# Reordering the steps, GpSimd shares, gathers and loads of a three-layer interaction network

## What is computed

```python
e = stack([tbl_f[ids[:, f]] for f in range(32)], axis=1)       # 512 x 32 x 16
x0 = xk = e
for W in (W0, W1, W2):                                         # 32 x (32 or 64) x 64
    xk = relu(einsum('bmd,bhd,mhk->bkd', x0, xk, W))           # 512 x 64 x 16
    outs.append(sum(xk, axis=2))
h = concatenate([*outs, dense_ctx], axis=1)                    # 512 x 208
y = relu(relu(h @ W_top1 + b1) @ W_top2 + b2) @ W_top3
```

## Time and profile before

| | before |
|---|---|
| median of 3 runs | 338.52 us |
| profiled execution: its time / its span | 339.5 us / 337.7 us |
| granted TensorE clock, mean | 0.98 |
| TensorE matmul busy | 309.4 us (92%) |
| VectorE busy | 268.5 us (80%) |
| GpSimd busy | 240.6 us (71%) |
| ScalarE busy | 63.1 us (19%) |
| DMA, mean rate over the span | 188 GB/s |

### The profile page before, as it was taken

The page is one execution under the profiler, slowest core; times in us unless marked ns, Lnnn a source line. Parts: engine busy times, 40 slices in busy tenths (PEclk is TensorE's granted clock), DMA queues, the critical chain, the costliest instruction groups (busy, mean ns, idle before and its releaser), DMA issues.

```text
span 337.7 us, 4699 instructions
## 1 busy us (share of the span) xinstructions
PE 309.4 (92%) x1828; PEld 128.8 (38%) x1828; DVE 268.5 (80%) x162; ACT 63.1 (19%) x103; POOL 240.6 (71%) x186
## 2 busy tenths in 40 slices
PE   0469999878989998989999999999999999999997
PEld 0435456434545353323333333333333333333334
DVE  0128579937996699999999999999998979999210
ACT  1030322122113410101221301131132012020011
POOL 5677777777777358899979797979958577649200
PEclk9998999995899999999999999999999999999999
DMA  6366647366398409696979696915998995230000
GB/s 176 106 178 175 214 109 224 73 170 203 98 308 304 156 10 320 213 307 196 325 246 308 247 322 200 330 45 151 317 363 259 320 284 135 36 103 1 2 0 0
DMA packets 31356, 63.60 MB, mean 188 GB/s; under 512 B 5606, under 2 KB 13030, under 8 KB 31334
## 3 DMA queue, kind: packets, MB, share of 16 engines
q1 hardware_dynamic: 20614, 52.28, 46.7%
q10 hardware_dynamic: 6624, 9.96, 10.1%
q0 software_dynamic: 4096, 1.06, 3.3%
HBM read 51.35 MB, written 1.71 MB: 157 GB/s over the span
## 4 chain that ended last, share of the span: by engine, by line
PE 58%; DMA 5%; DVE 2%; issue 1%; ACT 0%; SPq 0%; DVEq 0%
PE acc L951 51%; DMA fields_sb<-fields 5%; DVE vz L741 2%; PE factor L996 2%; PE acc L964 1%; PE factor L906 1%; PE factor L991 1%; PE factor L1003 1%; PE acc L996 1%; PE factor L1037 0%; PE acc L1074 0%; ACT factor L787 0%; SPq L611 0%; DVE feats L751 0%; DVE vz L772 0%
## 5 line engine op out<-in xcount | busy, mean ns | idle before, releaser
L741 DVE TENSOR_TENSOR vz<-fields_sb,factor 128x1024 f32<-128x1024 f32 (+3 forms) x113 | 230.5, 2089 | 31.9 <-PE factor L906 15.6
L951 PE MATMUL acc<-vz,w_sb 128*64 128x512 f32 (+1 forms) x1152 | 216.3, 514 | 7.9 <-DVE vz L741 7.2
L669 POOL DMA_INDIRECT gathered<-in_table,index x128 | 121.7, 951 | 38.4 <-issue 36.0
L686 POOL TENSOR_TENSOR pz<-fields_sb,hidden 128x1024 f32<-128x1024 f32 (+1 forms) x52 | 118.1, 2295 | 33.0 <-DMA hidden<-relu_out 9.5
L951 PEld LDWEIGHTS acc<-vz,w_sb 128*64 128x64 f32 x1152 | 82.2, 140 | 127.3 <-issue 89.9
L951 PE MATMUL acc<-pz,w_sb 128*64 128x512 f32 (+1 forms) x208 | 50.6, 578 | 0.0
L853 ACT ACTIVATE relu_out<-acc 128x512 f32<-128x512 f32 (+1 forms) x30 | 15.5, 516 | 109.9 <-PE acc L951 104.3
L787 ACT ACTIVATE factor<-hidden 128x1024 f32<-128x1024 f32 (+1 forms) x23 | 20.1, 879 | 59.7 <-DMA hidden<-relu_out 38.1
L741 DVE TENSOR_TENSOR vz<-rotated,factor 128x2048 f32<-128x2048 f32 x10 | 22.5, 2279 | 5.3 <-ACT factor L787 5.3
L951 PEld LDWEIGHTS acc<-pz,w_sb 128*64 128x64 f32 x208 | 15.0, 137 | 28.8 <-issue 26.5
L751 DVE TENSOR_REDUCE feats<-relu_out 128x32 f32<-128x512 f32 (+1 forms) x30 | 17.1, 570 | 6.6 <-ACT relu_out L853 6.5
(11 more groups left out here) (30 smaller groups left out, 43.0 us busy)
## 6 DMA issues: line engine op xcount, KB each, us to landing
fields_sb<-fields SPq DMA_DIRECT2D x48, 512.0 KB, 5.5
rotated<-fields SPq DMA_DIRECT2D x20, 512.0 KB, 6.7
fields_sb<-fields SPq DMA_DIRECT2D x32, 256.0 KB, 3.6
hidden<-relu_out ACTq DMA_DIRECT2D x30, 256.0 KB, 5.8
own<-fields SPq DMA_DIRECT2D x5, 512.0 KB, 3.6
gathered<-in_table,index POOLq DMA_INDIRECT x128, 3.7
hidden<-relu_out ACTq DMA_DIRECT2D x16, 128.0 KB, 3.8
fields<-gathered SPq DMA_DIRECT2D x5, 256.0 KB, 4.9
```

Source lines behind the costliest of these rows:

```text
L669: nc.gpsimd.indirect_dma_start(gathered[:, pair % GRING, j, :], None, table, bass.IndirectOffsetOnAxis(ap=index[:, i:i + 1], axis=0)).then ...
L686: nc.gpsimd.tensor_tensor(pz[:, at % PRING, 0:cols], fields[s][:, t, col:col + cols], hidden_of(step, g), ALU.mult).then_inc(pz_ready, 1)
L741: nc.vector.tensor_tensor(vz[:, at:at + nt, 0:cols].rearrange("p t (a n) -> p t a n", n=half), src[:, t:t + nt, col:col + cols].rearrange( ...
L951: last = nc.tensor.matmul(acc_of(step, ab), weights[:, kt, :], z[:, ab * half:(ab + 1) * half], start=start and j == 0, stop=stop and j == ...
```

## The change

Only tables and one constant change: the order BEGUN, the sets SPREAD, HALF and PAIRED, the shares POOL_TILES, the places of the gathers, the waits PACED and BEHIND_SPREAD on gathers, the order LOADS, and the place at which ScalarE makes the own squares of layer 0.

- BEGUN: (0, 2) comes ahead of (2, 0), (0, 3) ahead of (1, 1), and (0, 4) ahead of (2, 1) rather than behind (2, 2). (0, 6) comes ahead of (2, 4), (0, 7) ahead of (2, 5), and (2, 6) ahead of (0, 8).
- SPREAD and HALF: five spreads of both halves become four, seven of one half become six.
- GpSimd's tiles: 52 become 56. Two narrow steps that had a share, (1, 1) with 1 and (2, 3) with 3, have none, (1, 3) has 1, and the wide steps have 55 rather than 48; (1, 4) has 4 rather than 1, (2, 8) has 6 rather than 3.
- PAIRED: in (2, 2) the tiles are contracted alternately into the two halves of the accumulator, in one matmul of 512 columns instead of two of 256; ScalarE copies the accumulator out (`fold`), and TensorE adds the halves (`join`) before the relu.
- PACED gives 84 gathers a wait, BEHIND_SPREAD 8.
- LOADS: the scratch of block 3 ahead of that of block 2, that of block 5 ahead of that of block 4, and that of block 6 ahead of the fields of block 5.

```diff
-BEGUN = [(0, 0), (1, 0), (0, 1), (2, 0), (0, 2), (1, 1), (1, 2), (0, 3), (2, 1), (1, 3), (2, 2), (0, 4), (0,
+BEGUN = [(0, 0), (1, 0), (0, 1), (0, 2), (2, 0), (0, 3), (1, 1), (1, 2), (0, 4), (2, 1), (1, 3), (2, 2), (0,
...
-SPREAD = [(1, 0), (2, 3), (1, 4), (1, 5), (1, 9)]
-HALF = [(1, 1), (2, 0), (1, 2), (1, 3), (2, 4), (1, 7), (2, 7)]
+SPREAD = [(1, 0), (1, 3), (2, 2), (1, 7)]
+HALF = [(2, 0), (1, 1), (1, 2), (1, 5), (2, 4), (2, 5)]
...
-FIRST_GATHERS = 21
-GATHERS_IN = {(1, 1): (14,), (2, 3): (48, 0, 1), (1, 4): (2,), (1, 5): (10, 0, 0, 2, 0), (2, 4): (3, 0, 0),
+FIRST_GATHERS = 40
+GATHERS_IN = {(1, 3): (29,), (1, 4): (21, 6, 1, 0), (1, 5): (3, 0, 0, 2), (2, 4): (0, 1, 3), (2, 5): (3, 4, 1,
...
-PACED = {}
+PACED = {11: 2, 12: 2, 13: 2, 14: 2, 15: 3, 16: 3, 17: 4, 18: 4, 19: 3, 21: 3, 22: 2, 24: 6, 25: 3, 26: 4, 27:
...
-PAIRED = []
+PAIRED = [(2, 2)]
...
-            due.append((COLUMNS[VECTOR.index((step, 0))] + TURN_LAG, "own", step, 0))
+            due.append((COLUMNS[VECTOR.index((step, 0))], "own", step, 0))
```

## The result

The kernel after takes **336.70 us** (median of 12 runs, 334.56 to 338.02) against 338.64 for the kernel before in the same comparison: a ratio of 0.9933, 95% interval 0.9903 to 0.9962, so it is faster, by 1.9 us between the medians. 334.1 was forecast: the direction was right, the size less than half. Medians are over all runs of a kernel; the ratios leave out single slow runs, such as one of 1344.38 us among the twelve of the kernel before. The profiled execution of after took 337.33 us with a span of 335.5; before 339.5 and 337.7.

A forecast was written before the change was run, and what follows sets the result against it. TensorE's start of (1, 5) and its work from there bound the kernel, with GpSimd at (1, 4) the new bound. -5.5 - 1.1 + 2.2 = -4.4 gave 335.1 profiled, 334.1 median; range 330.3 to 338.9, own range 332 to 336.3.

The forecast's parts named there:

- TensorE reaches (1, 5) at 140.3: End of (1, 4): GpSimd's products set TensorE's start of (1, 5), at 140.3 rather than 145.81, 5.5 us earlier.
- gives gather 68 at 91.1, the product of (1, 3): GpSimd's queue at 1.25 per gather, walked on to the four products of (1, 4), ending 121.9, 131.6, 135.1 and 137.5.
- Without these waits (1, 4) would end near 136.5: TensorE in (1, 4): it waits for GpSimd about 3 us in all; otherwise the step ends near 136.5.
- The rule on the clock: TensorE's half rate would move rather than vanish; priced at +1.0, with only VectorE late.
- Head: VectorE ahead of (1, 5): begins (2, 0) at 41.7, (1, 1) at 55.3, (2, 1) at 79.2, ends (2, 3) at 121.5.
- rival C: 63 gathers up to number 96: new waits stretch the issue gap, 0.14 more each gives 342.9; chance 0.12.
- Rival A: At (1, 4) GpSimd is no bound: it ends at 136.5, 328.1 at most, 331 likelier; chance 0.14.
- From (1, 5) on: From (1, 5) to the perceptron: TensorE's work, 173.5 before, changes by -1.1 and +2.2.
- +2.2: GpSimd late by 0.7 at the first product of (1, 5), 1.5 at the fifth of (2, 5); bounds nothing and 5.
- -1.1: TensorE from (1, 5) on: one spread fewer, -1.07.
- Rival B: GpSimd's late products in (1, 5) to (1, 7) hold the loads of fields 6 and 7: 337.6; chance 0.18.
- PAIRED and LOADS: PAIRED at (2, 2) costs 0; LOADS delays block 2's fields to about 51 to 60, used at 64, not in the sum.

The follow-up runs named there:

- experiment 11: Kernel after without waits on gathers, two gathers moved from ahead of (1, 5)'s first product to ahead of (1, 4)'s second: 337.55 us.
- experiment 4: Kernel after with four entries in the ring of relu outputs instead of three: 335.47 us.
- experiment 2: Kernel after with PACED and BEHIND_SPREAD emptied, so no waits on gathers: 334.91 us.
- experiment 3: Kernel after with ten idle matmuls on TensorE ahead of the contraction of (0, 2), their values overwritten: 335.83 us.
- experiment 9: Kernel after with the old order LOADS: 336.36 us.
- experiment 5: Kernel after with experiments 1, 2 and 3 together: 334.18 us.
- experiment 10: Kernel after with experiments 1 to 4 together: 334.03 us.
- experiment 8: Kernel after without waits on gathers and with (0, 4) put back behind (2, 2): 338.57 us.
- experiment 7: Kernel after with PAIRED emptied, so (2, 2) has neither fold nor join: 336.67 us.
- experiment 1: Kernel after with the one product of (1, 3) moved from GpSimd to VectorE, its 29 gathers put into (1, 4): 336.01 us.

## Why the prediction was right and wrong

**TensorE reaches (1, 5) at 140.3: failed, 142.55.** The mechanism was right. In eight profiles the start of (1, 5) follows GpSimd's first product of (1, 4) by 20.95 to 21.00 us, whatever made that product early or late, and two gathers more put 2.48 us into that distance (experiment 11). What failed is the step at which the queue alone "gives gather 68 at 91.1, the product of (1, 3)", with nothing down for its hidden operand, and with it the times of the four products of (1, 4): 139.6 for 137.5. Of the 2.1 us 0.4 are gather 11, 1.25 late instead of 0.8. 1.7 are the wait for the hidden copy. My walk has no relu of (0, 4) between the squares and the copy, and so overlooks that it must wait for the entry of the relu ring, hence for the spread of (1, 3), hence for VectorE; and it puts nothing down for the four relays between relu and copy, which took 4.94 us to issue. The wait is gone with a fourth entry (experiment 4) and in the profiles of the same ring with 1.00 at 42 us (experiments 2 and 3), and it is 0.24 us where the relays took 3.43 (experiment 9).

**"Without these waits (1, 4) would end near 136.5": wrong by the prediction's own prices.** 16 tiles at 0.863 are 13.8 us, and behind VectorE's first unit at 124.8 they end at 138.6. The runs show this distance as 13.77 us. In after it makes 140.50, so even without GpSimd's waits (1, 5) would have been 0.2 later than forecast.

**"GpSimd holds (1, 4) at 140.3 anyway": failed.** The rule on the clock was priced at +1.0 on the ground that only VectorE would be late. Half rate at 42 us came true, in six of the nine profiles without idle matmuls, and it moved GpSimd too, through the very copy above. In the profile of after this is 1.7 us at (1, 5); in that of experiment 9 GpSimd waits 0.24. I weighed it as a thing that happens or not, while it comes and goes between executions.

**Head.** The start of (2, 0) was forecast 1.1 too late, the waits behind (0, 4) were right: 4.88 ahead of (2, 1) for 4.8, none at (0, 5). With the clock at 1.00 VectorE starts (2, 1) at 78.39, for 79.2.

**Waits on gathers, rival C: false.** The pitch is 1.25 with them. What they cost is 1.2 us at gather 11, for 0.8 forecast (by the medians 1.8 without the fourth relu output and 1.0 with it). **Rival A** was false as well: GpSimd did bound (1, 4), and it was out of the way only in experiments 5, 10 and 8. It was also priced too high: ahead of (1, 5) it could give 140.3 - 138.6 = 1.7 us, not 3.8.

**From (1, 5) on: right in sum, its parts not shown.** 174.65 for 174.6. The forecast +2.2 was to be waits for `pz` in (1, 5), (2, 5) and (1, 7). In after TensorE waits once for `pz`, 0.43 at 145.71, and 0.70 for VectorE at 278.74; the chain gives that one back to the last gathers of block 9 (223.41), its scratch and its loads. The rest is a gap of 0.11 at 185.38, and next to nothing elsewhere. TensorE is busy for 173.37 us of this part, against 173.53 before, and idle for 1.28, against nothing. By this count the terms are -0.2 and +1.3 rather than -1.1 and +2.2, though the ends of matmuls are modelled, so that part of a pause can be counted as work. That one spread fewer is worth 1.07 was not tested by itself. In the other eleven profiles the part takes 173.1 to 175.0 us. So the agreement of the sum to 0.05 us is luck. In the walk itself, from (1, 5) to (2, 5) the tables give 12 products and 20 gathers, not 16 and 23; the 53 us fit the former (28.2 + 25).

**Rival B** (337.6), late products that hold the loads of fields 6 and 7, did not show: between 146 and 278 us TensorE waited for no unit by more than 0.11. **PAIRED and LOADS** were rightly put at nothing (experiments 7 and 9). The earlier place of the own squares wasn't tried.

**The path in numbers**, for the profiled executions: -3.3 at (1, 5), for -5.5; +1.1 behind it, for +1.1; a span 2.2 shorter, for 4.4. The median, 336.70, is just above the forecast's own range of 332 to 336.3.

## What to carry to other kernels

Follow every instruction of the helper engine ahead of a bound, not only its queue: a product waited for a copy, the copy stood behind a relu and four DMA issues, and the relu behind a ring entry, three waits none of which was on the engine that I walked through. When a step is moved early on one engine, check each ring it passes for who must have read the entry by then. Hold a time without waits against the bare work of the step behind its first unit. And where a pause of TensorE makes a half rate possible, forecast a share of runs, and price it at every engine that is fed from there.

## What the runs showed that was not expected

- The stretch 42 to 50 us had 0.79 in six profiles and 1.00 in six, three of these with idle matmuls in the pause. The length of the pause ahead of it doesn't tell which: it was 1.94 in experiment 1, at full clock, and 1.92 in experiment 9, at half rate behind it. A mean granted clock of 0.994 or 0.995 stood for a half rate at 42 us in one profile, between 20 and 30 in another, between 94 and 98 in a third: only the stretches tell where it was.
- Four relays at the same place of the program took ScalarE from 3.31 (experiment 4) to 6.21 us (experiment 5) to issue, and a copy queued behind them waits that long (5.02 in after).
- A wait on a gather whose semaphore has long been reached costs nothing: 1.25 us from gather to gather with and without.
